# An attention and mixture-of-experts layer: the last chunk's shared expert behind the routed tiles, another order in the last group, and queries and keys turned once and spread by on-chip transfers

## The reference

```python
x = x + attention(layernorm(x))          # ternary weights in both projections
h = layernorm(x)
scores = sigmoid(h @ w_router); top_vals, top_idx = top_k(scores, 2)
out = sum over the two experts e of weight_e * ((silu(h @ w1[e]) * (h @ w3[e])) @ w2[e])
shared = silu(h @ ws1) * (h @ ws3) @ ws2
x = x + out + shared
```

## Time and profile before

| what | us |
|---|---|
| median of 3 runs (595.45 to 596.68) | 596.61 |
| the profiled execution, its own time | 590.83 |
| its span, from first to last instruction | 589.0 |
| PE busy / ACT busy / DVE busy in the span | 490.4 / 364.2 / 340.9 |
| PE's share of the chain of work that ended last | 58% |

### The profile page before, as it was taken

How to read it: one execution, slowest core, us unless ns; L and a number is a source line. 1 busy time by engine, 2 the same in 40 slices (tenths; PEclk the granted TensorE clock), 3 DMA queues, 4 the chain that set the end, 5 groups by cost and what they waited for, 6 DMA issues and landing times.

```text
span 589.0 us, 10118 instructions
## 1 busy us (share of the span) xinstructions
PE 490.4 (83%) x3328; PEld 276.6 (47%) x3328; DVE 340.9 (58%) x972; ACT 364.2 (62%) x567; POOL 166.8 (28%) x221
## 2 busy tenths in 40 slices
PE   1586889997999999999989888939697979999930
PEld 1583323233333333333334333417585869998920
DVE  6975566843581235812246766364967757666626
ACT  4253778883899878998777867535452335555520
POOL 4501101011101021010242227125455834444430
PEclk9887989897999999999999999779799899999975
DMA  8999999000000000000132003122011333444349
GB/s 230 299 304 306 279 7 2 2 1 1 1 1 1 1 2 1 1 0 1 37 99 86 26 1 114 45 85 73 15 60 48 94 101 101 125 124 120 110 139 344
DMA packets 66390, 49.84 MB, mean 85 GB/s; under 512 B 24552, under 2 KB 64072, under 8 KB 66344
## 3 DMA queue, kind: packets, MB, share of 16 engines
q1 hardware_dynamic: 62936, 39.89, 30.1%
q0 software_dynamic: 3408, 9.34, 4.4%
HBM read 19.88 MB, written 29.34 MB: 84 GB/s over the span
## 4 chain that ended last, share of the span: by engine, by line
PE 58%; DVE 16%; issue 11%; ACT 4%; POOL 4%; DMA 4%; SPq 1%; ACTq 0%; POOLq 0%; DVEq 0%
PE ps L1479 18%; PE ps L1459 12%; PE ps L1662 6%; PE ps L1443 5%; PE ps L1680 3%; ACT prob L696 3%; PE ps L1608 2%; PE ps L1488 2%; PE ps L1409 2%; DVE qk L973 2%; PE ps L1684 2%; POOL rows_by_expert L580 1%; PE ps L1671 1%; DMA yfin<-pair_out 1%; PE ps L1653 1%
## 5 line engine op out<-in xcount | busy, mean ns | idle before, releaser
L696 ACT ACTIVATE prob<-ps 128x1024 f32<-128x1024 f32 (+3 forms) x320 | 262.3, 916 | 85.3 <-PE ps L1459 84.3
L1479 PE MATMUL ps<-prob,v_sb 128*32 128x512 f32 (+3 forms) x1280 | 157.9, 567 | 12.2 <-POOL prob L539 8.5
L1459 PE MATMUL ps<-qk 50*128 50x512 f32 (+3 forms) x640 | 120.4, 441 | 8.9 <-ACT prob L696 5.6
L539 POOL TENSOR_SCALAR_AFFINE_SELECT prob<-prob 128x512 f32<-128x512 f32 x64 | 41.2, 645 | 253.4 <-ACT prob L696 253.2
L1459 PEld LDWEIGHTS ps<-qk 50*128 50x128 f32 x640 | 53.7, 193 | 92.8 <-ACT prob L696 69.1
L973 DVE CAST qk<-ps 128x512 fp32r<-128x512 f32 (+1 forms) x48 | 33.1, 691 | 68.7 <-PE ps L1443 68.7
L1479 PEld LDWEIGHTS ps<-prob,v_sb 128*32 128x32 f32 x1280 | 25.8, 110 | 57.6 <-issue 28.7
L641 POOL DMA_INDIRECT pair_out<-yo,xg x39 | 37.4, 959 | 54.3 <-DVE yo L1345 54.0
L1443 PE MATMUL ps<-ident,stack 128*128 128x128 f32 x192 | 33.0, 297 | 10.5 <-DVE qk L973 8.5
L1443 PEld LDWEIGHTS ps<-ident,stack 128*128 128x128 f32 x192 | 21.2, 146 | 42.6 <-issue 41.7
L1608 PE MATMUL ps<-x2T,ws_hi 128*128 128x512 f32 (+1 forms) x96 | 32.4, 420 | 5.1 <-DVE hid L1214 5.1
(11 more groups left out here) (205 smaller groups left out, 802.7 us busy)
## 6 DMA issues: line engine op xcount, KB each, us to landing
rows_by_expert<-pads SPq DMA_DIRECT2D x9, 1935.0 KB, 20.6
xg<-rows_by_expert SPq DMA_DIRECT2D x39, 129.0 KB, 2.2
yfin<-pair_out SPq DMA_DIRECT2D x8, 512.0 KB, 7.0
stage<-in_w SPq DMA_DIRECT2D x8, 352.0 KB
x_sb<-in_x SPq DMA_DIRECT2D x4, 512.0 KB, 6.2
res<-in_x SPq DMA_DIRECT2D x4, 512.0 KB, 4.0
out<-y_sb SPq DMA_DIRECT2D x4, 512.0 KB, 5.2
stage<-in_w SPq DMA_DIRECT2D x8, 176.0 KB
```

The costliest lines, as they stand in the source:

```text
L539: nc.gpsimd.affine_select(out=t, in_=t, compare_op=ALU.is_ge, fill=0.0, base=0, pattern=[[0, HPG], [1, P]], channel_multiplier=-1).then_in ...
L696: nc.scalar.activation(prob[:, u % NPB, 2 * hf:2 * hf + 2, c0:CH], ps[:, b:b + 2, c0:CH], ACT.Exp, scale=SCALE).then_inc(exp_done, 1)
L1459: ins = M(ps[:, 2 * (n % NSB) + h, c0:CH], qk[rows, par, PAIRS, kt * P:(kt + 1) * P], qk[rows, par, hf, j * CH + c0:(j + 1) * CH], start=T ...
L1479: ins = M(ps[VW * h:VW * (h + 1), O_BANK, c0:CH], v_sb[:, kt, :], prob[:, u % NPB, h, c0:CH], start=(kt == 0), stop=(u == LAST_OF[j]), ski ...
```

## The change

It has four parts.

1. *Queries and keys.* `stack` and `split` are gone. After `rotate`, PE turns the rotated 80 columns of a chunk (4 query heads and the key head, straight from `wk_b`) in one round of 4 transposes instead of three; DVE takes the round in two operations, high part and low part, into `qT` (`take_round`). SP then copies 16-row pieces of `qT` to their places in `qk` with 18 transfers of 32 KB per chunk, and 4 more per group for the shift rows, turned once at the start (`move`). PE waits for them by `ld_qk[j]` at the first unit of a chunk. The ones that face the shift rows are written once by POOL.
2. *SP's queue.* The clearing transfers are spread: three behind the moves of group 0, six behind those of group 1 (and behind a wait for all scores of group 0), the numbering behind those of group 2.
3. *The last group.* The steps stand one unit earlier from unit 13 on; `scale_x2` now stands ahead of the next `copy_output` on DVE; pieces 7 and 8 are split after attention; POOL sends the first half of chunk 1's rows ahead of the masks of chunk 3.
4. *The end.* The shared expert's last three blocks, of chunk 3, run behind the last routed tiles. Low parts of the hidden blocks 5 to 8 and of most late pieces go from POOL to DVE.

```diff
-RPC = 3
-ROUNDS = RPC * NC
+ROUNDS = NC
+QK_MOVES = [3 * HPG + 6 + (HPG if c == 0 else 0) for c in range(NC)]
-SHARED_PIECES, EARLY_PIECES, POOL_PIECES = KD + 1, 9, 15
+SHARED_PIECES, EARLY_PIECES, POOL_PIECES, UP_PIECES = KD + 1, 7, 11, KD + 1 + 4 * KD
-NEXT_ROUNDS = {26 + r: [("round", 1, r)] for r in range(ROUNDS - 2)}
-NEXT_ROUNDS[NU - 1] = [("round", 1, r) for r in (ROUNDS - 2, ROUNDS - 1)]
+NEXT_ROUNDS = {28 + 2 * r: [("round", 1, r)] for r in range(ROUNDS)}
...
+    0: [("round", 0, 1)], 4: [("out", 0, 0)], 8: [("round", 0, 2)], 12: [("out", 0, 1)], 16: [("round", 0, 3)],
+    24: [("out", 0, 2)], **{30 + 2 * r: [("round", 1, r)] for r in range(ROUNDS)}, NU - 1: [("weights",)],
...
 AFTER = {
-    (0, 0): [("out", 0, 3), ("step", 5, 2)], (1, 0): [("step", 6, 2), ("step", 0, 3), ("step", 1, 3)],
-    (2, 0): [("step", 2, 3)], (2, 1): [("step", 3, 3)], (3, 0): [("step", 7, 2)],
-    (5, 0): [("step", 4, 3), ("step", 5, 3)], (6, 0): [("step", 6, 3)], (7, 1): [("step", 7, 3)],
+    (-1, 0): [("out", 0, 3)], (0, 0): [("step", 0, 3), ("step", 1, 3)], (1, 0): [("step", 2, 3), ("step", 3, 3)],
+    (3, 0): [("step", 4, 3), ("step", 5, 3), ("step", 7, 2)], (4, 0): [("step", 6, 3)], (5, 0): [("step", 7, 3)],
 }
+FLAT_FIRST = (NC - 1) * SH
...
+            def move(g, c):
+                sp.wait_ge(x_free, round_use(g, c))
+                par, cs = (g + 1) % 2, slice(c * CH, (c + 1) * CH)
+                for hf in range(2):
+                    for h in range(2):
+                        head, at = 2 * hf + h, SLOT * h
+                        for part, n in ((0, 0), (1, 1), (0, 2)):
+                            sp.dma_start(qk_f[at + n * HD:at + (n + 1) * HD, par, hf, cs],
+                                         qT_f[head * HD:(head + 1) * HD, part, cs]).then_inc(ld_qk[c], 16)
+                for h in range(2):
+                    for part, n in ((0, 0), (0, 1), (1, 2)):
+                        at = SLOT * h + n * HD
+                        sp.dma_start(qk_f[at:at + HD, par, PAIRS, cs], qT_f[HPG * HD:QKD, part, cs]).then_inc(ld_qk[c], 16)
...
+            def take_round(g, c):
+                next_use()
+                if not (isinstance(g, int) and g == 0):
+                    dve.wait_ge(ld_qk[c], 16 * QK_MOVES[c] * g)
+                hi, lo = (qT[0:QKD, part, c * CH:(c + 1) * CH] for part in range(2))
+                link(V.tensor_copy(hi, ps[0:QKD, X_BANK, :]))
+                V.tensor_tensor(lo, ps[0:QKD, X_BANK, :], hi.bitcast(F32), ALU.subtract).then_inc(x_free, 1)
...
+                    if hf == 0 and kt == 0:
+                        pe.wait_ge(ld_qk[j], 16 * QK_MOVES[j] * (g + 1))
...
             for i in range(TILES + 2):
...
+                if i >= TILES:
+                    up(FLAT_FIRST + i - TILES)
+            for n in range(FLAT_FIRST, FLAT):
+                down(n)
+                if n + 2 < FLAT:
+                    up(n + 2)
```

More of the change, by code:

```diff
@@ L407, in _ @@
+            sp.wait_ge(s_ready, 2 * NU)
+            clear_rows(3, blocks)
+            for c in range(NC):
+                move(2, c)
+            sp.wait_ge(zeroed, 16 * blocks)
+            for b in range(blocks):
                 sp.dma_start(rows_d[b * PADS * P:(b + 1) * PADS * P, ID:ID + 1].rearrange("(k p) c -> p k c", p=P),
@@ L799, in _ @@
                     tile_out_low(i - 2)
+                if i >= TILES:
+                    n = FLAT_FIRST + i - TILES
+                    silu(n)
+                    if n > FLAT_FIRST:
+                        hidden_high(n - 1)
+            for n in range(FLAT_FIRST + 2, FLAT):
+                silu(n)
+                hidden_high(n - 1)
+            hidden_high(FLAT - 1)
         @block.vector
@@ L1034, in _ @@
             rotate(0, NT)
-            split(1, 0, NT)
             group_scales(1, D // P)
             ternary(1, D // P)
-            take_rounds(0, 0, ROUNDS - 4)
+            for c in range(NC):
+                take_round(1, c)
             copy_output(0, NC - 1)
@@ L1244, in _ @@
             row_stats(0, LN)
+            scale_x2(0)
             output(g, 1)
[L1246 to L1247 removed]
             low_part(4, 0)
@@ L1359, in _, with finish @@
                     tile_out(i - 2)
-            for c in range(NC):
+                if i >= TILES:
+                    hidden(FLAT_FIRST + i - TILES)
+            def finish(c):
                 dve.wait_ge(ld_fin[c], 32)
@@ L1367, in _ @@
                 ins.then_inc(fin_ready, 1)
+            for c in range(NC - 1):
+                finish(c)
+                if c == 0:
+                    hidden(FLAT - 1)
+            take_shared(NC - 1)
+            dve.wait_ge(evicted, NC)
+            finish(NC - 1)
         @block.tensor
@@ L1640, in _ @@
             pe.wait_ge(piece_done, SHARED_PIECES)
-            for n in range(FLAT + 2):
-                if n < FLAT:
+            after((-1, 0))
+            for n in range(FLAT_FIRST + 2):
+                if n < FLAT_FIRST:
                     up(n)
```

361 lines of the change are left out of this document (184 added, 177 removed).

## The result

The changed kernel takes 691.06 us (median of 4 runs, 690.33 to 692.56), the kernel before 596.03 us (594.33 to 596.68) on the same chip: ratio 1.160, 95% interval 1.157 to 1.164. I had forecast 577.5 us. The sign was wrong, and by far.

A forecast was written before the change was run, and what follows sets the result against it. Prediction: PE bounds steady attention and routed tiles, reloading scattered rows the end. 17.3 - 8.5 - 11.8 + 0.5 - 17 + 0.7 = -18.8 took 590.8 to 572.0; with 5.8 for the median 577.8, given as 577.5 us, range 564 to 598.

The forecast's parts named there:

- The issue price: SP's queue: each transfer of the moves takes 0.44 us to issue, with bounds of 0.38 and 0.58.
- The rival at 0.70: SP's queue: moves cost more to issue; at 0.70 us each the sum is +21.6, 618 us; chance of dearer issue 0.13.
- Group 0, +17.3: Queries and keys of group 0: first scores later by 7 (chunk 1), 7.4 (chunk 2) and 2.9 us (chunk 3).
- The chain: Group 0: round, two DVE operations, 18 issues on SP and one landing take 12.1 us to a chunk's first scores.
- Fewer rounds, -8.5 and -11.8: Rounds for the next group, 4 instead of 12: -8.5 us in group 0, -11.8 in groups 1 and 2.
- Covered, but with 1.6 us to spare: Groups 1 and 2: moves hidden before the next group's scores; chunk 1 ready at 21.2 us, needed at about 22.8.
- "No cost" of the clears: SP's queue: the spread clears stand behind moves, never ahead of one that is due, and cost nothing.
- The start, 0: Up to the first scores: moves replace chunk 0's rounds, a later low part delays a projection; they cancel within 2 us.
- The last group, +0.5: Last group: wait for piece 8 goes, -2.9 us; copies behind the scaling cost +1.7 each; bounds -3 and +5.
- Between attention and tiles, -17: Stretch behind attention: chunk 3's places come at 440 instead of 456.8, tiles start at 461.5 instead of 478.5 us.
- pieces through two staging buffers, or DVE with its added low parts: Rival, behind attention: these become the bound, tiles start only half as much earlier, 586 us; chance 0.14.
- The end, +0.7: Behind the last tile: three blocks of 14.4 us hide beside 17 us of reloading; two DVE operations leave +0.7 us.

The follow-up runs named there:

- l1: Kernel before with parts 1 and 2 alone, the transfers of groups 2 and 3 left out: 614.1 us, ratio 1.042 to the kernel before.
- y2: y1 with half of the transfers of chunks 0 and 1 of each group issued by GpSimd's queue: 583.9 us, ratio 0.977 to the kernel before.
- m2: Changed kernel with half of group 0's transfers for chunks 1, 2 and 3 issued by ScalarE's queue: 692.6 us, ratio 1.161 to the kernel before.
- h1: Parts 1 and 2 alone, first three weight pieces loaded ahead of or between the last group's transfers, piece 3's conversion later: 644.6 us, ratio 1.091.
- m3: Changed kernel with GpSimd's two fills of the key tile moved behind its small steps: 688.5 us, one run.
- d1: Kernel before with parts 3 and 4 alone: 617.7 us, ratio 1.034; run again 619.4 us, ratio 1.039.
- t5: d1 with both the edits of t1 and t4: 601.2 us, ratio 1.007 to the kernel before.
- t1: d1 with the last group's output copies of chunks 1 and 2 ahead of the scaling again: 611.4 us, ratio 1.037 to the kernel before.
- t4: d1 with three stage buffers of 512 columns instead of two of 768 for the last eight weight pieces: 610.5 us, ratio 1.017.
- y1: Kernel before with only groups 1 to 3 turned once and spread by transfers, weight pieces loaded between these: 598.5 us, ratio 0.997.
- w1: Kernel before with one added wait of PE, for five small loads at the first scores of group 2: 608.2 us, ratio 1.019.
- h2: h1 with m2's split, clears in threes behind chunk 3's and group 2's transfers, and m3's edit: 645.7 us, ratio 1.078.

## Why the prediction was wrong, by its steps

- **The issue price.** I took 0.44 us; it measured 0.63, beyond the 0.58 that I gave as the upper bound. Both came from loads out of DRAM; no row of a transfer within the chip's memory stood in the trace. The step failed by its size, and its bound was no bound: with nothing comparable in the rows I should have let it reach further. (By my own numbers chunk 1 is late from 0.48 per issue on, not 0.50.) By my own rival's working 0.63 would have made the sum +9.5 us: group 0 10.3 and the three boundaries some 6 each more, 606 us: the price turns the sign, but is 85 us short of the 691 measured. The rival at 0.70 named the right place, SP's queue, and gave 618.
- **Group 0, +17.3.** PE waits 12.4, 13.1 and 7.1 us there. The chain was right: with 0.63 it gives 15.5 us from the round to the scores, and for chunk 1 the trace has 15.4 (58.87 to 74.22). The price and the slower clock behind each wait are missing in it (clock 0.73 in the stretch, against 0.89).
- **Fewer rounds, -8.5 and -11.8.** The size was right, 5.0 to 6.6 us a group where I had 5.4, by l1 and by y2 (outputs turned at 212.50 and 281.32, 68.8 us). In the changed kernel it is spent on waits of 5.4, 9.3, 2.0, 2.3 and 2.2 us and on slow matmuls. "Covered, but with 1.6 us to spare" fell with the price.
- **"No cost" of the clears.** Wrong: they lie ahead of group 2's transfers (twelve issues in 13.8 us instead of 7.5) and, in m2, of another queue's.
- **What was left out.** SP's queue carries the weight pieces behind the transfers. That is 24 us by h1, the largest single miss, and it has no step in my working at all: this is the step that failed first, a term put at nothing without a reason. I followed the moved instructions to who waits for them, and not to what stands behind them on their queue.
- **The start, 0.** +6.5 us: 3.4 of it the cast beside GpSimd's fills (m3). Of the rest, PE's waits of 2.67 us (ended by a low part that now stands behind the normalising, as the times have it: it ends at 47.47, PE goes on at 47.58) and 1.03 us (for a transfer) are what shows.
- **The last group, +0.5.** d1 makes it +13.8, and +10.9 when run again. The copies behind the scaling I priced at 1.7 us each; they made PE wait 3.45 and 3.91 us. What they cost in all is 2.6 to 7.4 us (t5 beside d1 again, t1 beside d1); the rest of this loss, some 6 to 8 us, stays open. The last mask wait did shrink, from 8.49 to 3.0 us.
- **Between attention and tiles, -17.** PE does have less to do (62.8 us busy instead of 70.3), but it was never PE alone that this stretch waited for. My rival "pieces through two staging buffers, or DVE with its added low parts" was the right one, at half its strength: I gave it 8.5 us less gain; d1 shows the whole gain gone and 6.7 us lost (8.6 when run again), t4 gives 8.5 of it back. The places of chunk 3 came 57 us behind the mask wait instead of the 44.6 that I had.
- **The end, +0.7.** +4.8 here and +7 in d1: the three blocks wait 4.9 us for their hidden parts in d1, beside slow matmuls. The cover was thinner than its 17 us looked.

What t5's remaining 4 us are, and why the last group takes 13 us longer than before in y1 and y2 as well, was not tried. That the clock makes each wait dearer is shown by w1 for one place; how much of group 0's loss it is was only argued.

## What to carry to other kernels

When work is moved onto a queue, list what stands behind it on that queue and who waits for that; the moved work's own consumer may be the smaller loss. Price many small transfers by their issue, and if no row shows one, let the bound reach far enough to change the sign. Taking work off an engine gains nothing in a stretch whose end hangs on a ring through other engines and two buffers: find the ring first.

## What the runs showed of the hardware

- Issuing a transfer of 32 KB (16 partitions of 2 KB) within the chip's memory takes 0.63 us on SP's queue, 0.66 on ScalarE's and 0.52 on GpSimd's; it lands 1.9 to 2.1 us later (medians in the changed kernel, m2 and y2).
- While transfers of 1.9 MB are being worked off, issues on another queue take 1.4 us each (m2), and 0.63 where they are ahead of them (h2).
- A wait of TensorE of 7.8 us in a stretch of steady work cost 10.3 to 11.9 (w1); the granted clock is 0.51 in the 10 us from 225 on behind it and 1.00 in the next 10.
- GpSimd's two fills of 128x2048, 3.54 us together, made a VectorE cast of 0.56 us take 3.90 (the changed kernel beside m3).
